# A grouped conv on TensorE: neighbours' taps taken on the output side, moved by one partition by DMA

## The reference, cut to what matters

```python
x = x + ffn0(cond0(x))          # cond0: per-sample 64x64 mixing matrix; ffn0: 1024x1024 base + gated LoRA
x = x + ffn1(cond1(x))

def cond1(x, c, weight, c_weight, bias):
    out = lax.conv_general_dilated(x, weight, window_strides=(1,), padding=[(4, 4)],
                                   dimension_numbers=('NCH', 'OIH', 'NCH'), feature_group_count=4)
    ctx = jnp.einsum('nd,od->no', c, c_weight)
    return out + ctx[:, :, None] + bias[None, :, None]

def ffn1(x, gate_w, base_w, base_b, lora_A, lora_B):
    weights, selected = jax.lax.top_k(x @ gate_w.T, 2)        # softmax over the two, expanded to w_full
    return x @ base_w.T + base_b + 2.0 * lora(x, w_full)      # 8 experts of rank 16
```

## Time and profile before

| what | us |
|---|---|
| median of 3 runs | 2255.09 |
| the profiled execution | 2255.57 |
| its span, first to last instruction | 2253.8 |
| TensorE busy in the span | 2211.0 |
| VectorE busy | 1389.7 |
| GpSimd busy | 857.7 |
| ScalarE busy | 401.5 |

### The profile page before, as it was taken

How to read it: one execution, slowest core, us unless ns; L and a number is a source line. 1 busy time by engine, 2 the same in 40 slices (tenths; PEclk the granted TensorE clock), 3 DMA queues, 4 the chain that set the end, 5 groups by cost and what they waited for, 6 DMA issues and landing times.

```text
span 2253.8 us, 41501 instructions
## 1 busy us (share of the span) xinstructions
PE 2211.0 (98%) x13452; PEld 2172.2 (96%) x13452; DVE 1389.7 (62%) x3667; ACT 401.5 (18%) x923; POOL 857.7 (38%) x1053
## 2 busy tenths in 40 slices
PE   4999999999999999999999999999999999999998
PEld 4999999999999999999999999999999999999998
DVE  6777777776777777776655555555555555555554
ACT  3221212222222222222211111111111111111110
POOL 5444343434343444444433333333333333333331
PEclk9999999999999999999999999999999999999999
DMA  4312111111212121212433333333343333333431
GB/s 167 112 63 71 68 69 70 69 70 69 70 63 76 59 79 59 79 59 92 116 94 92 88 87 87 87 87 95 99 93 91 88 87 87 87 87 97 100 92 59
DMA packets 134114, 189.48 MB, mean 84 GB/s; under 512 B 16080, under 2 KB 98384, under 8 KB 134096
## 3 DMA queue, kind: packets, MB, share of 16 engines
q1 hardware_dynamic: 133792, 188.69, 30.1%
q10 hardware_dynamic: 304, 0.56, 0.1%
HBM read 122.01 MB, written 67.18 MB: 84 GB/s over the span
## 4 chain that ended last, share of the span: by engine, by line
PE 96%; DVE 1%; DMA 1%; ACT 1%; issue 1%; POOL 0%; SPq 0%; DVEq 0%; ACTq 0%
PE psB L807 72%; PE psB L834 9%; PE psT L787 7%; PE psT L781 3%; PE psT L789 3%; PE psT L782 1%; PE psB L820 1%; DMA stage<-in_l0w 0%; POOL Wlo L324 0%; DVE small L666 0%; DMA outb<-in_condw 0%; ACT Whi L443 0%; DVE small L670 0%; POOL res L352 0%; DMA Xraw<-in_x 0%
## 5 line engine op out<-in xcount | busy, mean ns | idle before, releaser
L807 PE MATMUL psB<-Whi,Yhi 128*128 128x384 f32 (+2 forms) x3072 | 749.5, 352 | 5.4 <-issue 5.4
L333 POOL TENSOR_TENSOR Xlo<-Xraw,Xhi 128x256 fp32r<-128x256 f32 (+1 forms) x512 | 422.6, 855 | 791.1 <-ACT Xhi L417 791.1
L807 PE MATMUL psB<-Whi,Ylo 128*128 128x384 f32 (+2 forms) x3072 | 714.1, 341 | 0.0
L807 PE MATMUL psB<-Wlo,Yhi 128*128 128x384 f32 (+2 forms) x3072 | 710.0, 339 | 0.0
L807 PEld LDWEIGHTS psB<-Whi,Ylo 128*128 128x128 f32 x3072 | 559.3, 189 | 0.0
L807 PEld LDWEIGHTS psB<-Wlo,Yhi 128*128 128x128 f32 x3072 | 558.3, 189 | 0.0
L807 PEld LDWEIGHTS psB<-Whi,Yhi 128*128 128x128 f32 x3072 | 518.2, 190 | 21.9 <-issue 5.6
L566 DVE TENSOR_TENSOR Y<-psT,row 128x256 f32<-128x256 f32 x512 | 216.4, 423 | 339.2 <-PE psT L789 318.1
L362 POOL TENSOR_TENSOR res<-res,bias 128x256 f32<-128x256 f32 x256 | 181.3, 740 | 439.9 <-DMA res<-x_scratch 439.9
L431 ACT CAST Yhi<-Y 128x512 fp32r<-128x512 f32 x256 | 159.1, 622 | 896.8 <-DVE Y L568 896.8
L605 DVE TENSOR_TENSOR outb<-psB,res 128x384 f32<-128x384 f32 (+1 forms) x384 | 227.4, 677 | 89.3 <-PE psB L834 89.2
(11 more groups left out here) (85 smaller groups left out, 1436.4 us busy)
## 6 DMA issues: line engine op xcount, KB each, us to landing
Xraw<-in_x SPq DMA_DIRECT2D x64, 512.0 KB, 3.3
x_scratch<-outb SPq DMA_DIRECT2D x64, 512.0 KB, 2.7
Xraw<-x_scratch SPq DMA_DIRECT2D x512, 64.0 KB, 3.5
res<-x_scratch SPq DMA_DIRECT2D x64, 512.0 KB, 4.7
out<-outb SPq DMA_DIRECT2D x64, 512.0 KB, 3.0
row<-row_scratch SPq DMA_DIRECT2D x128, 64.0 KB, 3.1
stage<-in_l0w SPq DMA_DIRECT2D x8, 580.5 KB, 8.7
stage<-in_l1w SPq DMA_DIRECT2D x8, 580.0 KB, 6.7
```

The costliest lines, as they stand in the source:

```text
L333: last = pool.tensor_tensor(Xlo[:, piece], Xraw[:, par, piece], as_f32(Xhi[:, piece]), ALU.subtract)
L807: last = mm(psB[:, 3 * par + b, 0:cols], y, w[:, k, BANK0[b]:BANK0[b] + cols], start=(k == 0 and y is yh and w is Whi), stop=(b == 2 and k ...
```

## The change

The gather of layer 1 loads each octet unshifted, 128 columns a block, without pad columns. `CT` holds, instead of two passes, one table of 256 columns and its low part: the first 128 columns are the taps that fall into the same octet ("main"), the last 128 those that reach into the octet beside ("side": for positions t < 4 the part is owed to the octet above, for t >= 4 to the octet below). A block is three matmuls of 256 columns: Xhi against the high table, Xhi against the low table, Xlo against the high table. The main half is evacuated by VectorE in one sum with the row term. The side half is copied from `psT` into `side` by ScalarE (`copy_side`, once for each chunk; `side` lies in the memory of `mixT` and `prod`). For each half of the blocks (h = 0 after chunk 1, h = 1 after chunk 3) SP issues two transfers from `side` to `shifted` (`shift`): partitions 0 to 126 to 1 to 127 for t < 4, and partitions 1 to 127 to 0 to 126 for t >= 4. VectorE adds `shifted` to Y (`add_shifted`), half 0 ahead of the evacuation of chunk 3, half 1 ahead of `emit`. Yhi and Ylo of layer 1 are made by halves of blocks instead of halves of columns, so that each K-tile needs both halves; TensorE waits for both at k = 0. Ylo's second half is moved behind `emit`, and `high_ht` ahead of `high_x`. TensorE's mix of chunk c waits for the side copy of chunk c-2 in place of the evacuation. `shifted` is cleared once at the start.

```diff
...
+        shifted = sb("shifted", [P, 2, BR, HALF_B * GC])
...
-        Xraw = sb("Xraw", [P, 2, XW])
-        Xhi, Xlo = sb("Xhi", [P, XW], F32R), sb("Xlo", [P, XW], F32R)
+        Xraw = sb("Xraw", [P, 2, H])
+        Xhi, Xlo = sb("Xhi", [P, H], F32R), sb("Xlo", [P, H], F32R)
...
-        mixT = sb("mixT", [P, MODES, C])
-        prod = sb("prod", [P, MODES, C])
+        mixbuf = sb("mixbuf", [P, 2, MODES * C])
+        mixT, prod = (mixbuf[:, i, :].rearrange("p (k o) -> p k o", k=MODES) for i in range(2))
+        side = mixbuf[:, :, :].rearrange("p h (t n) -> p h t n", t=BR)
...
+        side_zero, side_out, side_in, y_sum = sem("side_zero"), sem("side_out"), sem("side_in"), sem("y_sum")
...
+        def y_half(ap, layer, h):
...
+            if layer == 0:
+                return ap[:, h * HB:(h + 1) * HB]
+            return ap.rearrange("p (t n) -> p t n", t=BR)[:, :, h * HALF_B * GC:(h + 1) * HALF_B * GC]
...
-                        first = 1 if r < PAD else 0
-                        sp.dma_start(dst[r * GC:(r + 1) * GC, :, first:first + Q], src[(r + PAD) % BR])\
-                            .then_inc(g_loaded[par], 16)
+                        sp.dma_start(dst[r * GC:(r + 1) * GC, :, :], src[r]).then_inc(g_loaded[par], 16)
...
-                        if lay == 0:
-                            sp.wait_ge(pad_zero, par + 1)
...
-                        sp.dma_start(to[:, :, 0, 0:r + 1, :], convw[:, :, BR - r:BR + 1, :]).then_inc(conv_in, 16)
-                        sp.dma_start(to[:, :, 1, r:BR, :], convw[:, :, 0:BR - r, :]).then_inc(conv_in, 16)
+                        t0, t1 = max(0, r - REACH), min(BR, r + REACH + 1)
+                        u0 = t0 + REACH - r
+                        sp.dma_start(to[:, :, 0, t0:t1, :], convw[:, :, u0:u0 + t1 - t0, :]).then_inc(conv_in, 16)
+                        if r < REACH:
+                            t0, t1, u0 = r + REACH, BR, 0
+                        else:
+                            t0, t1, u0 = 0, r - REACH + 1, BR + REACH - r
+                        sp.dma_start(to[:, :, 1, t0:t1, :], convw[:, :, u0:u0 + t1 - t0, :]).then_inc(conv_in, 16)
...
+                if lay1 == 1:
+                    for h in range(2):
+                        shift(*after(j, par), h)
...
+            def shift(j, par, h):
...
+                m = 2 * j + par - STEPS
+                sp.wait_ge(side_out, NC * m + 2 * h + 2)
+                if isinstance(m, int) and m == 0:
+                    sp.wait_ge(side_zero, 1)
+                else:
+                    sp.wait_ge(y_sum, 2 * m + h - 1)
+                sp.dma_start(shifted[1:P, h, 0:REACH, :], side[0:P - 1, h, 0:REACH, :]).then_inc(side_in, 16)
+                sp.dma_start(shifted[0:P - 1, h, REACH:BR, :], side[1:P, h, REACH:BR, :]).then_inc(side_in, 16)
...
+            pool.memset(shifted[:, :, :, :], 0.0).then_inc(side_zero, 1)
...
-                if isinstance(j, int) and n in (STEPS - 2, STEPS - 1):
...
-                    pool.wait_ge(x_hi, n + 1)
-                    pool.wait_ge(x_lo, n + 1)
-                    pool.wait_ge(res_ready, n + 1)
-                    v = Xraw[:, par, :].rearrange("p (b q) -> p b q", b=BG)
-                    pool.memset(v[:, :, 0:QP:Q], 0.0).then_inc(pad_zero, 1)
...
-                    pool.tensor_tensor(CT[:, :, :, 1, :], craw, as_f32(CT[:, :, :, 0, :]), ALU.subtract)\
+                    pool.tensor_tensor(CT[:, :, 1, :, :], craw, as_f32(CT[:, :, 0, :, :]), ALU.subtract)\
...
-                nc.scalar.copy(Xhi[:, 0:w], Xraw[:, par, 0:w]).then_inc(x_hi, 1)
+                nc.scalar.copy(Xhi[:, :], Xraw[:, par, :]).then_inc(x_hi, 1)
...
-                    act.wait_ge(y_chunk, NC * n + (2 * h + 2 if layer == 0 else NC))
-                    nc.scalar.copy(Yhi[:, par, h * HB:(h + 1) * HB], Y[:, h * HB:(h + 1) * HB])\
-                        .then_inc(yhi_half, 1)
+                    if layer == 0:
+                        act.wait_ge(y_chunk, NC * n + 2 * h + 2)
+                    else:
+                        act.wait_ge(y_sum, 2 * (n - STEPS) + h + 1)
+                    nc.scalar.copy(y_half(Yhi[:, par, :], layer, h), y_half(Y[:, :], layer, h)).then_inc(yhi_half, 1)
...
+            def copy_side(j, par, c):
...
+                m = 2 * j + par - STEPS
+                act.wait_ge(y_chunk, NC * (m + STEPS) + c + 1)
+                if isinstance(m, int) and m == 0:
+                    act.wait_ge(agg_ready, STEPS)
+                else:
+                    act.wait_ge(side_in, 64 * m + 32 * (c // 2) - 32)
+                bank = psT[:, c % 2, :].rearrange("p (b s t o) -> p b s t o", b=2, s=2, t=BR)
+                to = side[:, c // 2, :, :].rearrange("p t (b o) -> p b t o", b=HALF_B)
+                b = 2 * (c % 2)
+                nc.scalar.copy(to[:, b:b + 2], bank[:, :, 1]).then_inc(side_out, 1)
...
-                if last_of_0:
-                    for k in range(KT // 2):
-                        split_w(k, 1)
+                for c in range(NC):
+                    if last_of_0:
+                        split_w(c, 1)
+                    if lay1 == 1:
+                        copy_side(*after(j, par), c)
...
+                if lay1 == 1 and lay0 is not None:
+                    high_ht(*before(j, par))
...
-                if lay0 is not None:
+                if lay1 != 1 and lay0 is not None:
...
-                    nc.scalar.copy(CT[:, :, :, 0, :], craw).then_inc(s_hi, 1)
+                    nc.scalar.copy(CT[:, :, 0, :, :], craw).then_inc(s_hi, 1)
...
+                        bank = psT[:, c % 2, :].rearrange("p (b s n) -> p b s n", b=2, s=2)
...
-                        add = bcast(row[:, par, :], 1, 2)
-                        parts = (bank[:, :, 0, :], bank[:, :, 1, :])
+                        nc.vector.tensor_tensor(y, bank[:, :, 0, :], bcast(row[:, par, :], 1, 2), ALU.add).then_inc(y_part, 1)
+                        dve.wait_ge(y_part, NC * n + c + 1)
+                        nc.vector.tensor_tensor(y, bank[:, :, 1, :], y, ALU.add).then_inc(y_chunk, 1)
...
+                        bank = psT[:, c % 2, :].rearrange("p (b s t o) -> p b s t o", b=2, s=2, t=BR)
...
-                        parts = tuple(bank[:, :, s, :].rearrange("p b (t o) -> p b t o", t=BR) for s in range(2))
-                    nc.vector.tensor_tensor(y, parts[0], add, ALU.add).then_inc(y_part, 1)
-                    dve.wait_ge(y_part, NC * n + c + 1)
-                    nc.vector.tensor_tensor(y, parts[1], y, ALU.add).then_inc(y_chunk, 1)
+                        nc.vector.tensor_tensor(y, bank[:, :, 0], add, ALU.add).then_inc(y_chunk, 1)
...
+            def add_shifted(j, par, h):
...
+                m = 2 * j + par - STEPS
+                dve.wait_ge(side_in, 64 * m + 32 * h + 32)
+                dve.wait_ge(y_chunk, NC * (m + STEPS) + 2 * h + 2)
+                y = y_half(Y[:, :], 1, h)
+                nc.vector.tensor_tensor(y, shifted[:, h, :, :], y, ALU.add).then_inc(y_sum, 1)
...
             def split_y(j, par, layer, halves):
...
-                    dve.wait_ge(y_chunk, NC * n + (2 * h + 2 if layer == 0 else NC))
...
-                    nc.vector.tensor_tensor(Ylo[:, par, h * HB:(h + 1) * HB], Y[:, h * HB:(h + 1) * HB],
-                                            as_f32(Yhi[:, par, h * HB:(h + 1) * HB]), ALU.subtract)\
-                        .then_inc(ylo_half, 1)
+                    nc.vector.tensor_tensor(y_half(Ylo[:, par, :], layer, h), y_half(Y[:, :], layer, h),
+                                            as_f32(y_half(Yhi[:, par, :], layer, h)), ALU.subtract).then_inc(ylo_half, 1)
...
+                if lay1 == 1:
+                    add_shifted(*after(j, par), 0)
...
-                if lay1 is not None:
+                if lay1 == 0:
...
+                if lay1 == 1:
+                    add_shifted(*after(j, par), 1)
...
+                if lay1 == 1:
+                    split_y(*after(j, par), lay1, range(1, 2))
...
-                if not (isinstance(n, int) and n == 0 and c < 2):
+                if layer == 1 and not (isinstance(j, int) and n == STEPS and c < 2):
+                    pe.wait_ge(side_out, NC * (n - STEPS) + c - 1)
+                elif not (isinstance(n, int) and n == 0 and c < 2):
...
-                        g = k % G
-                        for w in range(2):
-                            xs = slice(k * QP + w, k * QP + w + Q)
-                            mm(to, Xhi[:, xs], CT[:, g, w, :, :].rearrange("p s n -> p (s n)"),
-                               start=(w == 0), stop=False)
-                            last = mm(to[:, 0:P], Xlo[:, xs], CT[:, g, w, 0, :], start=False, stop=(w == 1))
+                        hi, lo = (CT[:, k % G, s, :, :].rearrange("p w n -> p (w n)") for s in range(2))
+                        mm(to, Xhi[:, xs], hi, start=True, stop=False)
+                        mm(to, Xhi[:, xs], lo, start=False, stop=False)
+                        last = mm(to, Xlo[:, xs], hi, start=False, stop=True)
...
```

(5 more changed lines are left out.)

## The result

The changed kernel takes 3666.55 us (median of four, 3665.38 to 3668.08) against 2255.06: the ratio is 1.626, with a 95% interval of 1.624 to 1.629. It is slower by 1411 us, 22.05 us for each of the 64 tiles of the second layer. The forecast was slower, 4458 us, with a range of 3350 to 5200.

A forecast was written before the change was run, and what follows sets the result against it. TensorE's stream bounds the kernel at 18.09 us a step; two serial one-engine moves make it 7.15 + 1.21 + 19.3 + 1.75 + 19.3 + 3.8 = 52.5, so 64 x 34.4 more gives 4458 us, range 3350 to 5200.

The forecast's parts named there:

- S to M1: TensorE, from a step's first base matmul to the end of its second mix chunk: 7.15 us, including 2.6 slow restart.
- move 0: SP's two 127-row transfers for half 0, on one DMA engine: 19.3 us from issue to both landed.
- move 1: SP's two 127-row transfers for half 1, issued only after half 0 is added and chunk 3 evacuated: 19.3 us.
- Part 1: TensorE's conv: 24 matmuls of 256 columns at 0.12 us replace 32 pairs at 0.116, saving 0.83 us a step.
- Part 3: Ylo's last half behind emit on VectorE: the next step starts 0.17 us late, leaving 0.66 of 0.83 saved.
- Part 2: VectorE loses 1.7 us and gains 1.4; ScalarE gains four side copies, 1.5 us; free as work, not as chain links.
- B: Rival: transfers dealt over all DMA engines, landing in 2.2 to 3 us; step 17.43 us, 2213 us, faster; chance 0.06.
- M+1.56: Time claimed for the second half's issue on SP, counted from the end of TensorE's fourth mix chunk.
- Part 4: Partition shift by DMA: two moves in series on the chain, with VectorE, ScalarE and SP work queued behind; 19.3 us each.
- The break-even of 3.6 us: Landing time of the second half's issue at which the step equals today's; the step is 14.53 plus landing beyond 2.9.
- C: Rival: transfers dealt out but landing late, 4.7 us, from sharing SP's queue; step 19.23 us, 2329 us; chance 0.04.
- D: Rival: one DMA engine, each packet waiting for the one before, 120 ns each; 78.9 us a step, 6150 us; chance 0.04.

The follow-up runs named there:

- the kernel that came out ahead: Changed kernel with moves cut 112 rows SP, 15 ScalarE, semaphore per half, chunk 3 evacuated first, Ylo before emit, mix one tile earlier: 2211.46 us, ratio 0.981.

## Why the prediction was right, and where its number was off

**The way and the case.** The bound was read rightly: TensorE's stream sets the time until another chain is longer than 18.09 us, and the two moves in a row are that chain. Of the two cases for 127 rows, one engine was the right one. The step that carried it was the one from "16 short packets for each of 363 transfers" to equal shares, and 127 being prime. From the trace of before alone this was an inference, since the transfers counted there have 16, 64 or 128 rows; the row counts in the experiments settle it.

**The number.** The step was put at 52.5 us, and it is 40.1 on the mean (18.09 + 22.05). In the step shown:

| term | predicted, us | measured, us |
|---|---|---|
| S to M1 | 7.15 | 7.46 (6.07 in the step after it) |
| M1 to the first issue | 1.21 | 1.14 |
| move 0 | 19.3 | 13.70 |
| sum, evacuation, copy, gap | 1.75 | 1.46 |
| move 1 | 19.3 | 13.62 |
| sum, emit, Ylo, restart | 3.8 | 3.23 |

In this step 11.3 of the 11.9 us too many lie in the moves, and there in one factor: 68 ns for a packet of 1 KB, where it took 46. The fixed part of 2.0 us was right. The 68 was drawn on a line between packets of 512 B, read from HBM, and of 4 KB, half of them read from HBM and half stored to it. The short ones cost 53 ns there, which is no price of bytes; from SBUF to SBUF 1 KB costs 46 ns and halving the bytes nearly halves it. The lower bound, bytes alone at 40 ns, came nearest, since it has no small reads in it; the middle was taken between rows of which one did not apply.

**The slow clock.** It was put at 2.6 us a step from one restart near the start. In the changed kernel the granted clock falls during both idle stretches and comes back some us after work begins:

```profile
1905.00:1910.00 5.00, 0.00 (x0) 0.00 (x0) 0.49 (x1) 0.00 (x0) 0.00 (x0) 0.73 0.05 18
1910.00:1915.00 5.00, 2.13 (x7) 2.13 (x8) 4.57 (x17) 0.82 (x2) 0.00 (x0) 0.50 0.40 123
1915.00:1920.00 5.00, 5.00 (x27) 5.00 (x26) 0.54 (x2) 0.37 (x1) 2.14 (x4) 0.75 0.86 199
1920.00:1925.00 5.00, 5.00 (x34) 5.00 (x33) 0.74 (x2) 0.75 (x2) 0.68 (x1) 1.00 0.06 16
```

0.50 is 1.2 GHz, 1.00 is 2.4. S to M1 is 4.55 by the prediction's own count, so the clock cost 2.9 us in one step and 1.5 in the next: over these two the mean is 2.2, near the term of 2.6. (In the kernel without moves S to M1 is 4.70, from 1505.56 to 1510.26; by that it is 2.8 and 1.4.)

**Part 1** holds: the new mix runs at 0.12 us a matmul, and the kernels without moves save 0.68 and 0.76 us a step, where 0.66 and 0.83 were worked out. By columns alone there would have been no saving. **Part 3** had the right sign and about twice the size. **Part 2** holds as a statement about work: without moves TensorE waits for none of the four copies.

**The rivals.** B, dealt over all engines, was priced at 2213 us, and that price was wrong by its own steps. With 14 engines the kernel takes 2259.5. Two terms were wrong: the issue, 0.77 to 0.82 us where 0.35 had been taken (the second issue at M+1.56 is 1.21 and 0.35), and the chain of chunk 3, which I had started at its own time although Part 4 itself says that it queues behind the sum of half 0. The break-even of 3.6 us of landing for the second issue was therefore far too generous: landing was 2.4 to 2.6 us and the kernel stood just above break-even. Had the transfers been dealt out, the right forecast would have been "no change", not faster. C's landing of 4.7 us did not occur in that kernel. D, packets one after the other at 120 ns, is refuted by the 46 ns.

## What to carry to other kernels

Look at the outer count of both sides of a transfer before its bytes: a move by one partition is 127 rows, a prime, and runs on one DMA engine, at 13.7 us for two such transfers of 1 KB rows, where 112 + 15 rows on 16 and 15 engines take 4.2. The profile shows it without any timing, by the number of packets under 512 B that each transfer adds. And when a result must go round through DMA between two products of a saturated TensorE, price every link of that loop against the time that TensorE leaves it, issues and the order of its own engine's queue included. In the kernel that came out ahead the producer also stood earlier in the step; how much of the gain is owed to that was not separated.

## What the runs showed of the hardware that was not expected

One DMA engine moves SBUF to SBUF at 22 GB/s (46 ns for 1 KB) with about 2.0 us around it. SP's issue of such a transfer takes 0.6 us for 127, 124 or 122 rows (1, 2 and 4 engines) and 0.5 to 0.6 for 112 rows (16 engines), but 0.8 for 126 rows and 0.82 to 0.85 for 15 rows (14 and 15 engines), where the transfers of 128 rows to or from HBM take 0.34 to 0.39. When two transfers of 127 rows share one engine and one queue, the second issue takes 1.08 us (the median is 1.14); from two queues it does not (0.58 and 0.61), and the packets of the two queues alternate on that engine.
